# Second attention of a macaron block: one square root of u(u+1) instead of two square roots, for every second head pair

## The reference

```python
diff_sq = jnp.maximum(q_norm_sq + k_norm_sq - 2.0 * qk, 0.0)
denom = jnp.maximum((1.0 - CURV * q_norm_sq) * (1.0 - CURV * k_norm_sq), 1e-06)
cosh_arg = jnp.maximum(1.0 + 2.0 * CURV * diff_sq / denom, 1.0)
distance = jnp.where(cosh_arg > 1.0, jnp.arccosh(jnp.maximum(cosh_arg, 1.0 + 1e-12)), 0.0)
attn = jax.nn.softmax(-distance, axis=-1)
out = jnp.einsum('bhnm,bhmd->bhnd', attn, v)
```

## Time and profile before

| | us |
|---|---|
| median of 3 runs | 3040.18 (3038.32 to 3042.1) |
| time of the profiled execution | 3041.84 |
| its span, first to last instruction | 3040.1 |
| busy over the span: PE / DVE / ACT / POOL | 2598.1 / 2307.1 / 2223.2 / 1637.9 |
| mean granted clock of PE | 0.864 |

### The profile page before, as it was taken

The page is one execution under the profiler, slowest core; times in us unless marked ns, Lnnn a source line. Parts: engine busy times, 40 slices in busy tenths (PEclk is TensorE's granted clock), DMA queues, the critical chain, the costliest instruction groups (busy, mean ns, idle before and its releaser), DMA issues. The chain is left out here.

```text
span 3040.1 us, 42347 instructions
## 1 busy us (share of the span) xinstructions
PE 2598.1 (85%) x12208; PEld 1727.1 (57%) x12208; DVE 2307.1 (76%) x4329; ACT 2223.2 (73%) x2497; POOL 1637.9 (54%) x1288
## 2 busy tenths in 40 slices
PE   7999979999799996999975878778687777589998
PEld 6877756666587774878852323223232232268887
DVE  7677756777566777898977788787787877498887
ACT  5555536656455555777849999999999999777776
POOL 4667642122266763545536676776756667334444
PEclk9999979999899997999976667766666767689999
DMA  3111111111111112111100000000000000021111
GB/s 134 42 56 41 41 23 41 44 43 43 51 42 56 41 41 96 45 43 45 51 0 1 1 1 1 0 1 1 1 1 1 1 1 1 22 92 56 42 55 42
DMA packets 24917, 101.62 MB, mean 33 GB/s; under 512 B 5856, under 2 KB 7904, under 8 KB 15680
## 3 DMA queue, kind: packets, MB, share of 16 engines
q1 hardware_dynamic: 23360, 99.51, 9.5%
q10 hardware_dynamic: 1408, 0.34, 0.0%
HBM read 82.33 MB, written 2.62 MB: 28 GB/s over the span
## 5 line engine op out<-in xcount | busy, mean ns | idle before, releaser
L1911 POOL TENSOR_TENSOR A_Y<-A_Y,A_U 128x2048 f32<-128x2048 f32 x86 | 390.0, 4558 | 222.1 <-ACT A_U L1958 222.1
L1994 DVE TENSOR_SCALAR A_U<-ps 128x1024 f32<-128x1024 f32 x256 | 309.0, 1217 | 127.0 <-POOL A_Y L1911 58.1
L2000 DVE SCALAR_TENSOR_TENSOR A_U<-ps,A_U 128x1024 f32<-128x1024 f32 x256 | 310.8, 1214 | 57.3 <-PE ps L2144 57.3
L2144 PE MATMUL ps<-A_QT,A_KT 9*128 9x512 f32 x512 | 180.8, 702 | 193.6 <-DVE A_U L2000 162.0
L477 POOL TENSOR_TENSOR F0b_h<-F0b_h,dn 128x512 f32<-128x512 f32 x128 | 212.0, 1661 | 111.9 <-DVE F0b_h L409 111.8
L477 POOL TENSOR_TENSOR F0a_h<-F0a_h,dn 128x512 f32<-128x512 f32 x128 | 212.1, 1662 | 104.6 <-DVE F0a_h L409 104.5
L2144 PEld LDWEIGHTS ps<-A_QT,A_KT 9*128 9x128 f32 x512 | 65.7, 252 | 329.6 <-DVE A_U L2000 237.4
L1911 POOL TENSOR_TENSOR dn<-dn,A_U 128x2048 f32<-128x2048 f32 x42 | 190.3, 4551 | 112.8 <-ACT A_U L1958 112.8
L1958 ACT ACTIVATE A_U<-A_U 128x2048 f32<-128x2048 f32 (+1 forms) x96 | 236.5, 2464 | 0.0
L2116 PE MATMUL ps<-A_Y,A_VA 128*32 128x512 f32 x688 | 228.9, 799 | 5.8 <-DVE A_OT L1893 3.0
L1350 DVE CUSTOM_DVE_ANT_0 ps<-ps,A_mask 128x256 f32<-128x256 f32 (+1 forms) x512 | 184.8, 421 | 58.6 <-PE ps L1430 57.8
(11 more groups left out here) (417 smaller groups left out, 8134.7 us busy)
## 6 DMA issues: line engine op xcount, KB each, us to landing
dn<-weight_rows SPq DMA_DIRECT2D x32, 1024.0 KB, 4.6
F1a_cwb<-weight_rows SPq DMA_DIRECT2D x16, 1024.0 KB, 4.6
F1b_cwb<-weight_rows SPq DMA_DIRECT2D x16, 1024.0 KB, 4.6
A_KZ<-A_KT SPq DMA_DIRECT2D x132, 48.0 KB
A_QZ<-A_qs SPq DMA_DIRECT2D x96, 64.0 KB, 2.0
dn<-in_down SPq DMA_DIRECT2D x2, 2048.0 KB, 12.2
stage<-in_up SPq DMA_DIRECT2D x1, 2560.0 KB, 13.8
X<-in_x SPq DMA_DIRECT2D x4, 512.0 KB, 7.0
```

Source lines behind the costliest of these rows:

```text
L1911: eng.tensor_tensor(flat(y_slot(m, h)), flat(y_slot(m, h)), flat(Um[:, h % UR]), ALU.add).then_inc(s["t_ready"], 1)
L1994: eng.tensor_scalar(u_step(n), d_pair(n), 0.0, None, ALU.max).then_inc(s["dp_vector"], 1)
L2000: eng.scalar_tensor_tensor(out=u, in0=g_pair(), scalar=CLAMP, in1=u, op0=ALU.min, op1=ALU.mult).then_inc(s["u_ready"], 1)
L2144: last = eng.matmul(ps[:, 4 + b, :], KT[r:r + 9, pair, kt * P:(kt + 1) * P], QT[r:r + 9, pair, :], start=True, stop=True)
```

## The change

Every second pair of a chunk (`ONE_ROOT = (1, 3, 5, 7)`, the second pair of each burst) takes another way. DVE makes y = u(u+1) from u, one head at a time (`product`: 128 x 2048, both inputs in SBUF), directly after the last scale of the burst; it waits for `pvh_done` (the slot of Y is free) and tells ACT by the new semaphore `v_ready`. ACT takes one root of y in place, one head at a time, and leaves u as it is. POOL's add then gives u + sqrt(u(u+1)), and ACT takes Ln with scale 2 and bias 1, and Exp with scale -1. The first pair of each burst and POOL's program stay as they were.

```diff
+                            def one_root(h):
+                                y = flat(y_slot(m, h))
+                                eng.wait_ge(s["v_ready"], products_by(c, h) + 1)
+                                eng.activation(y, y, ACT.Sqrt).then_inc(s["s_ready"], 1)
...
+                            for g in range(SETS):
+                                for pair in (2 * g, 2 * g + 1):
+                                    if pair in ONE_ROOT:
+                                        one_root(2 * pair)
+                                        one_root(2 * pair + 1)
+                                    elif pair % 2 == 0:
+                                        two_roots(2 * pair, 1)
+                                        two_roots(2 * pair + 1, 1)
+                                    else:
+                                        two_roots(2 * pair, 2)
                                 eng.preload_act_table_set("natural_log_exp_and_others")
...
+                                    if pair in ONE_ROOT:
+                                        eng.activation(y, y, ACT.Ln, bias=1.0, scale=2.0)
+                                    else:
+                                        eng.activation(y, y, ACT.Ln)
                                     eng.drain()
-                                    eng.activation(y, y, ACT.Exp, scale=-2.0).then_inc(s["y_exp"], 2)
+                                    eng.activation(y, y, ACT.Exp,
+                                                   scale=-1.0 if pair in ONE_ROOT else -2.0).then_inc(s["y_exp"], 2)
...
+                            def product(h):
+                                u = flat(Um[:, h % UR])
+                                eng.drain()
+                                if not first or h >= YR:
+                                    eng.wait_ge(s["pvh_done"], c * PAIRS + h // 2 - 1)
+                                eng.scalar_tensor_tensor(out=flat(y_slot(m, h)), in0=u, scalar=1.0, in1=u, op0=ALU.add,
+                                                         op1=ALU.mult).then_inc(s["v_ready"], 1)
...
                                     scale(n0 + i)
+                                    pair = 2 * g + i // TPC
+                                    if i % TPC == TPC - 1 and pair in ONE_ROOT:
+                                        product(2 * pair)
+                                        product(2 * pair + 1)
                                     after(i)
```

More of the change, by code:

```diff
@@ L103, in macaron @@
                           "recip_ready", "xa_ready", "xv_ready", "turned", "d_done", "g_done", "dp_vector", "u_ready", "s_ready",
-                          "t_ready", "y_exp", "pvh_done"]
+                          "t_ready", "y_exp", "v_ready", "pvh_done"]
             sems[n] = {k: sem(f"{n}_{k}") for k in kinds}
@@ L1607, in attn1 @@
                 TURN = 3
+                ONE_ROOT = (1, 3, 5, 7)
                 def y_number(m, h):
@@ L1621, in y_two, with products_by @@
                     return two.rearrange("p n t q -> p (n t q)")
+                def products_by(c, h):
+                    return c * (2 * len(ONE_ROOT)) + 2 * len([n for n in ONE_ROOT if n < h // 2]) + h % 2
                 def u_two(h):
@@ L1948, in main @@
                                     turned_scalar(eng, i, first_bank(i))
[L1949 to L1958, removed]
-                                eng.preload_act_table_set("natural_log_exp_and_others")
[L1960 to L1963, removed]
@@ new lines, in free_slot, with two_roots @@
+                            def free_slot(h):
+                                if not first or h >= YR:
+                                    eng.wait_ge(s["pvh_done"], c * PAIRS + h // 2 - 1)
+                            def two_roots(h, n):
+                                y = y_two(m, h) if n == 2 else flat(y_slot(m, h))
+                                u = u_two(h) if n == 2 else flat(Um[:, h % UR])
+                                free_slot(h)
+                                eng.wait_ge(s["u_ready"], c * STEPS + TPC * (h // 2 + 1))
+                                eng.activation(y, u, ACT.Sqrt, bias=1.0)
+                                eng.activation(u, u, ACT.Sqrt).then_inc(s["s_ready"], n)
@@ new lines, in one_root @@
+                            def one_root(h):
[12 more added lines that the diff above has]
+                                        two_roots(2 * pair, 2)
+                                eng.preload_act_table_set("natural_log_exp_and_others")
+                                for pair in (2 * g, 2 * g + 1):
+                                    y = y_two(m, 2 * pair)
+                                    eng.wait_ge(s["t_ready"], c * H + 2 * pair + 2 + UR)
+                                    if pair in ONE_ROOT:
+                                        eng.activation(y, y, ACT.Ln, bias=1.0, scale=2.0)
+                                    else:
+                                        eng.activation(y, y, ACT.Ln)
```

## The result

The changed kernel takes 3183.26 us in the median of 4 runs (3182.53 to 3184.32), against 3040.2 for the kernel before: a ratio of 1.0471, 95% interval 1.0453 to 1.0489. Slower, as forecast (3173); the profiled execution has a span of 3181.9 us, 141.8 more.

What follows compares the result with a forecast made beforehand. ACT looked like the bound before, DVE after: its line of 118.5 + 18.4 - 1.6 = 135.3 us per chunk plus 12.3 of port waits, 17.8 more than before; times 7.5 chunks, 133 us, gives 3173 us, range 3100 to 3207.

Steps and rivals of the forecast that it cites:

- DVE's reserve of 11.1 us per chunk: DVE's waits for POOL in a 129.6 us chunk, taken as its only room; the other 118.5 is its own line.
- The port: DVE's products and POOL's adds lock each other out of SBUF for whole instructions: 12.3 us of waits per chunk.
- the hand count: Queues of DVE, ACT and POOL carried forward through one chunk's four bursts; the next burst 0 starts at 147.2 us.
- The slot of Y costs no wait: Before the products: PE's weighted sum frees the slot ahead of the factor the last scale already waited for; no wait.
- that it would meet at any pace: DVE's short waits for PE, 0.5 to 2.3 us each, counted as fixed within its own line of 118.5 us.
- since PE transposes while DVE multiplies: The 0.81 us wait for PE's first transpose, ahead of two of four bursts, is covered by products: -1.6 us per chunk.
- The chunk, 147.4 forecast: Length of one chunk: DVE's line of 135.3 us plus 12.3 of port waits, some 147.4, 17.8 more than before.
- DVE is the new bound, and what ACT gains becomes idle time: DVE's line of 135.3 us per chunk exceeds the 121.6 of POOL and ACT, so ACT's saved 14.4 gain nothing.
- 7.5 chunks: First burst has no extra in front, the last no burst behind: 7.5 chunks of 17.8 us, 133 us.
- no conflict at the port: Rival, 8 in 100: the same tensor is read once, so products meet nothing; only DVE's line counts, 3083 us.
- the faster case: Rival, 5 in 100: ACT's gain comes through, POOL's chain of 121.6 us per chunk is the bound, 2980 us.
- PE falls behind: Rival, 5 in 100: PE's clock may sink, its waits grow by up to a third, 4 us per chunk, 3205 us.

Runs made afterwards that it cites:

- ACT's half alone: Changed kernel without DVE's products, ACT taking one root of u for every second pair (wrong values): 2990.16 us, ratio 0.9827 to the kernel before.
- the run with memsets: Changed kernel with POOL's adds replaced by memsets of about the same duration (wrong values): 3105.59 us, ratio 1.0208 to the kernel before.
- the run with the cast ahead: Changed kernel with the products of pairs 5 and 7 moved behind the first of DVE's four casts that follow them: 3182.47 us, ratio 1.0463.
- without the port: Changed kernel with memsets for POOL's adds: 3105.59 us, chunk 138.0; with products of pairs 5 and 7 also behind the first cast: 3083.5 us, chunk 135.5.
- joined products: Changed kernel with both heads' products in one instruction of 4096: 3181.04 us, ratio 1.0462 to the kernel before.
- shortening ACT: Changed kernel without the Exp of each group's first pair on ACT (wrong values): 3160.8 us, ratio 1.04 to the kernel before.
- both roots: Changed kernel with products made and waited for, but ACT taking both roots of every head as before: 3240.98 us, ratio 1.0651.

## Why the prediction was right, point by point

- **What bounds the kernel before**: ACT, with DVE's reserve of 11.1 us per chunk close behind. ACT's half alone (-52 us) and a chunk of 123.4 (121.6 forecast) bear it out.
- **The product**: 2.28 us forecast, 2.29 measured, in all 64 where nothing is in the way (the run with memsets). The same tensor read twice is held like two.
- **The port**: shown by the run with memsets, at 78 us of 143. Forecast 12.3 us per chunk; the products' waits are 9.5 over all chunks (76.0 / 8) and 8.3 in the five that give the 148.0, so this term was too large by 2.8 to 4.0. By bursts 0 to 3, the hand count had 4.7, 0.1, 4.4 and 3.1, and 1.6, 1.3, 5.0 and 1.7 were measured.
- **The slot of Y costs no wait**: right, no wait of the products names PE.
- **PE's waits "that it would meet at any pace", and its transposes covered "since PE transposes while DVE multiplies"**: this step failed. PE gets three of four transposes done beside the products; the fourth waits for the first cast, which stands behind them, and the weighted sums wait with it. The first halves of bursts 0 and 3 cost 12.4 + 12.6 - 2 x 9.8 = 5.4 us per chunk, 2.7 per burst. That the cast's place is the cause, the run with the cast ahead shows (9.7 each). Of the 2.7 us, 1.6 are sums that run at the lower clock (5.3 in place of 3.63). It is not the mere loss of DVE's waits for POOL ahead of these bursts (3.96 and 1.86 us in the earlier trace rows): with ACT's half alone all of DVE's waits for POOL are down from 90.0 to 26.0 us, and these halves take 10.0 and 10.3.
- **The chunk, 147.4 forecast and 148.0 measured**: so close by luck. In the five chunks measured the port's waits are 4.0 us under the forecast, the first halves 5.1 over it (5.4 over six chunks), the second halves 0.8 under. The sum itself is a little loose: 135.3 + 12.3 is 147.6, and the hand count ends at 147.2.
- **"DVE is the new bound, and what ACT gains becomes idle time"**: this reading failed, though the queues carried forward by hand, which held all three engines, came near the right length. DVE's line is 135.5 to 138 us, and was measured as such only without the port. With the port, a product waits for the adds of the same group's first pair, and so three of four groups are a ring over DVE, ACT and POOL of 36.4 us. Shortening DVE's work (cast, joined products) gave nothing, shortening ACT gave 22 us, lengthening ACT (both roots) cost 58. The hand count did contain the ring, since it let ACT's and POOL's times follow from the product before; I read only DVE's column of it.
- **7.5 chunks**: 141.8 / 18.4 is 7.7.
- **The rivals**: no conflict at the port is excluded (maximum 6.43 us for 2.29 of work), the faster case too. That PE falls behind came in part, by its order and by its clock together. The stage's mean clock, 0.69 to 0.67, hides it: the sums ahead of bursts 0 and 3 ran 45% longer (5.3 against 3.63), more than the third that this rival had. With 5.4 us per chunk the size was near the 4 of that rival, which the forecast had left out; the smaller waits at the port made room for it.
- **The signs named for the profile after** (ACT at 75%, L1994's waits gone, products from 2.29 to 6.4, some adds of 6.5) all came.

What was not tried: a product with one input in ps. The banks that it could read are being written by PE at that time.

## What to carry to other kernels

Before moving work to the engine that looks idler, take its reserve from the waits that end on its own line, not from its busy share, and ask which engine waits for the small work that the new instruction pushes back (here PE, for a cast), and whether that engine then runs at a lower clock. If the added instruction reads two tensors from SBUF on VectorE while GpSimd works on SBUF inputs, price it as work of both engines, once plus up to one whole instruction of the other: here 2.29 us of work took up to 6.43 beside adds of 4.55. And when an edit takes time from an engine and the waits grow by as much, stop trimming that engine: look for the ring through the others, and test it by shortening the one that idles.

## What the runs showed of the hardware

- The product (two SBUF inputs) runs at 2.29 us beside memsets of 1.81, which only write; beside an add, which reads, it waits. The Trainium skill (SBUF — State Buffer, section "SBUF: two separate sides") states that a VectorE instruction with two SBUF inputs contends for the shared port pair only with a GpSimd instruction that reads SBUF; by that, the runs agree.
- The norm's small var_eps, one input, is another case: with memsets in the kernel before it still took 885 to 1593 ns, where elsewhere it takes 170. My expectation of 0.17 was wrong. The one of 1.59 us ends at 1772.04, with the memset beside it (1772.02), so this small instruction is held by a GpSimd instruction that only writes.

```profile
L1862 DVE TENSOR_SCALAR var_eps<-mv x7: 885/1232/1593, 1770.5 to 2548.5; 128x4 f32<-128x4 f32 x7
```

```profile
1770.22 1.80 POOL L1913 MEMSET A_U<- 128x2048 f32 x1
```

```profile
1770.45 1.59 DVE L1862 TENSOR_SCALAR var_eps<-mv 128x4 f32<-128x4 f32 x1
```

- In a contest the engines take turns by whole instructions. In the changed kernel one product ends at 2273.27 and the next starts 0.09 us later; the waiting add gets in between (it starts at 2271.07, ends at 2277.63 after 6.56 us), and the second product takes 6.42. In the same way an add that meets a joined product takes 8.7 (up to 8.8).

```profile
2273.36 6.42 DVE L2034 SCALAR_TENSOR_TENSOR A_Y<-A_U 128x2048 f32<-128x2048 f32 x1
```

```profile
2271.07 6.56 POOL L1916 TENSOR_TENSOR A_Y<-A_Y,A_U 128x2048 f32<-128x2048 f32 x1
```

- Ahead of bursts 0 and 3, 16 weighted sums take PE 3.63 us at a granted clock of 1.00 (592 to 617 ns each). In the changed kernel they take 4.6 to 6.1 us: there the clock is at its lower level when they start, and the first ones take 1060 ns. A stage's mean clock (0.69 and 0.67) does not show this.
